# A gated cross-attention and MoE block on one core: sums of squares moved to ScalarE, unread products at the start, front work reordered

## The reference

```
x = x + tanh(g_xattn) * xattn(layernorm(x), ctx_2048, desc_router, W_q, b_q, itok)
x = x + tanh(g_ffn)   * moe(layernorm(x), gate_w, gate_b, fc1_w, fc1_b, fc2_w, fc2_b, alpha)

xattn: q = x @ W_q.T + b_q;  scores = q @ desc_router.T / 16, only the 4 sets listed for the token;
       the best 2 of them -> softmax weights over the 64 sets -> weights @ set_states
moe:   logits = x @ gate_w + gate_b; best 2 of 8 experts, softmax of the two, times alpha;
       for each of the 8 experts: gelu(x @ w1 + b1) @ w2 + b2, weighted and summed
layernorm(x) = (x - mean) / sqrt(var + 1e-5)
```

## Time and profile before

| | |
|---|---|
| three runs | 306.29, 307.38, 309.16 us |
| median | 307.38 us |
| profiled execution: span from the first to the last instruction | 304.3 us |
| profiled execution: time of its own beside the span | not given; the median is 3.1 us above the span |
| TensorE products busy | 251.6 us (83%) |
| VectorE busy | 213.1 us (70%) |
| ScalarE busy | 177.5 us (58%) |
| GpSimd busy | 147.2 us (48%) |
| mean granted TensorE clock | 0.907 |

### The profile page before, as it was taken

The page is one execution under the profiler, slowest core; times in us unless marked ns, Lnnn a source line. Parts: engine busy times, 40 slices in busy tenths (PEclk is TensorE's granted clock), DMA queues, the critical chain, the costliest instruction groups (busy, mean ns, idle before and its releaser), DMA issues.

```text
span 304.3 us, 9126 instructions
## 1 busy us (share of the span) xinstructions
PE 251.6 (83%) x3075; PEld 235.6 (77%) x3075; DVE 213.1 (70%) x701; ACT 177.5 (58%) x491; POOL 147.2 (48%) x122
## 2 busy tenths in 40 slices
PE   2999534241799999999999999999999999999910
PEld 2998433231689989999999999999999999989900
DVE  4899999896789778686677768677866555455500
ACT  2144878776574766856766685676666545555400
POOL 2121148994524556677545464454536355444240
PEclk9999855555599999999999999999999999999995
DMA  6999999996414444474534454455454536452320
GB/s 179 336 375 377 378 371 378 377 322 214 106 34 77 73 72 70 73 83 80 97 63 74 88 74 80 80 77 69 77 84 74 87 55 94 69 77 32 37 31 3
DMA packets 47262, 41.06 MB, mean 135 GB/s; under 512 B 23569, under 2 KB 43794, under 8 KB 47090
## 3 DMA queue, kind: packets, MB, share of 16 engines
q1 hardware_dynamic: 39088, 29.75, 33.0%
q0 software_dynamic: 7488, 10.39, 23.1%
q10 hardware_dynamic: 642, 0.33, 0.4%
HBM read 26.10 MB, written 9.37 MB: 117 GB/s over the span
## 4 chain that ended last, share of the span: by engine, by line
PE 60%; DVE 12%; DMA 6%; issue 3%; ACT 3%; POOL 1%; DVEq 0%; POOLq 0%; ACTq 0%
PE bank L615 30%; PE bank L631 29%; DMA out_dram<-xn,add_at 4%; DMA xs<-xrows,fetch_at 1%; DVE rows L1052 1%; DVE wreg L1061 1%; DMA xTp<-xs 1%; ACT wreg L806 1%; ACT rows L877 1%; DVE xs L1031 1%; DVE earlier L1105 1%; DVE wreg L1297 1%; DVE gmark L1095 1%; POOL out_dram L1529 1%; POOL xs L1521 1%
## 5 line engine op out<-in xcount | busy, mean ns | idle before, releaser
L615 PE MATMUL bank<-xTp,wreg 128*128 128x128 f16 x1872 | 155.3, 221 | 1.4 <-ACT xTp L866 0.7
L631 PE MATMUL bank<-wreg,rows 128*128 x936 | 150.5, 273 | 0.3 <-DVE rows L1434 0.3
L615 PEld LDWEIGHTS bank<-xTp,wreg 128*128 x1872 | 131.1, 99 | 9.6 <-issue 1.4
L877 ACT ACTIVATE rows<-bank,maskbias 128x128 f32<-128x128 f32 x312 | 88.9, 371 | 42.1 <-PE bank L615 21.6
L1529 POOL DMA_INDIRECT out_dram<-xn,add_at x39 | 66.7, 1711 | 88.1 <-DMA out_dram<-xn,add_at 48.8
L631 PEld LDWEIGHTS bank<-wreg,rows 128*128 128x128 f16 x936 | 79.1, 98 | 4.3 <-issue 0.4
L1432 DVE TENSOR_SCALAR rows<-rows 128x512 f16<-128x512 f32 x78 | 36.5, 468 | 41.6 <-ACT rows L877 41.5
L1521 POOL DMA_INDIRECT xs<-xrows,fetch_at x39 | 47.1, 1206 | 23.2 <-issue 11.3
L1434 DVE SCALAR_TENSOR_TENSOR rows<-rows 128x512 f16<-128x512 f32 x78 | 54.0, 693 | 2.7
L1297 DVE SCALAR_TENSOR_TENSOR wreg<-wreg (+1 forms) x16 | 36.7, 2292 | 13.9 <-ACT wreg L806 13.3
L885 ACT ACTIVATE xn<-xn,maskbias 128x256 f32<-128x256 f32 x39 | 20.0, 513 | 36.9 <-DVE xn L1423 36.8
(11 more groups left out here) (202 smaller groups left out, 208.0 us busy)
## 6 DMA issues: line engine op xcount, KB each, us to landing
wreg<-in_L_ffn_fc_w_dram SPq DMA_DIRECT2D x16, 1024.0 KB, 12.7
xrows<-rows SPq DMA_DIRECT2D x4, 528.0 KB, 6.4
xs<-in_x_dram SPq DMA_DIRECT2D x4, 512.0 KB, 9.3
out_dram<-xs SPq DMA_DIRECT2D x4, 512.0 KB, 9.1
xs<-in_L_ffn_fc_b_dram SPq DMA_DIRECT2D x1, 1024.0 KB, 5.7
xs<-xrows,fetch_at POOLq DMA_INDIRECT x39
out_dram<-xn,add_at POOLq DMA_INDIRECT x39
xTp<-xs SPq DMA_TRANSPOSE x38, 3.2
```

Source lines behind the costliest of these rows:

```text
L615: mm = pe.matmul(put, w, xT[:, i % NX, x_part, k, :], start=(k == 0 and n == 0), stop=(k == KC - 1 and n == 2))
L631: mm = pe.matmul(yb, h, w, start=(c == 0 and n == 0), stop=(c == FC - 1 and n == 2))
L877: op = act.activation(h32[i % 2][:, f * P:(f + 1) * P], bank[2 * (i % 2) + half][:, c * P:(c + 1) * P], ACT.Gelu, bias=b1cur[:, i % NX, f: ...
```

## The change

1. `norm1` is kept for group 0 alone. For groups 1 to 3 ScalarE runs a new `spread(g)`: four activations Square of the raw rows with bias minus the mean (from `xgate`) and the sum along the row into `var_sum`; VectorE's `variance1(g)` makes (sum + 256 eps)/256 of it in one operation. The power on GpSimd stays.
2. The minus mean comes from `xgate`, so `keep_gate` is moved ahead: for groups 1 to 3 it waits for the score products only, no longer for VectorE's reading of the bank. `score_pair(3, 0)` now waits for that reading instead.
3. TensorE starts with 20 products of `ones` (f16 view, 256 columns) into bank 3, which nobody reads; they wait for the memset of `ones`.
4. The context transposes go to banks 6 and 7 instead of 5 and 6, and TensorE waits for the mask only before attention(0).
5. The order of calls on TensorE, ScalarE and VectorE is another; on VectorE `norm1(0)` comes after the projection's part of `rhs_c`, and `variance1` and `weigh_sets(2)` are put between the halves of `add_attention`.

```diff
+        var_sum = sb("var_sum", [P, NT])
...
+        UNREAD = 20
...
             def score_pair(g, j):
...
-                if g >= 2 and j == 0:
-                    pe.wait_ge(xgate_ready, g - 1)
+                if g == 2 and j == 0:
+                    pe.wait_ge(xgate_ready, 2)
+                if g == 3 and j == 0:
+                    pe.wait_ge(scores_read, 2)
...
+            pe.wait_ge(ones_ready, 2)
+            for n in range(UNREAD):
+                pe.matmul(bank[3][:, 0:2 * P], ones[:, 0:P // 2].bitcast(F16), ones[:, :].bitcast(F16), start=True, stop=True)
             pe.wait_ge(pool_const, 1)
...
             pe.wait_ge(ctx_in, 16)
-            pe.wait_ge(mask_ready, 1)
             transpose_sets(0)
             score_pair(1, 0)
             transpose_sets(1)
+            score_pair(1, 1)
             transpose_pair(2, 0)
-            score_pair(1, 1)
+            transpose_pair(2, 1)
             pe.wait_ge(ctxT_sb, 2)
             set_gates((0, 1))
             score_pair(2, 0)
             set_gates((2, 3))
-            transpose_weights(0)
-            transpose_pair(2, 1)
-            attention(0)
             score_pair(2, 1)
             transpose_pair(3, 0)
             transpose_pair(3, 1)
+            transpose_weights(0)
+            pe.wait_ge(mask_ready, 1)
+            attention(0)
+            score_pair(3, 0)
+            score_pair(3, 1)
             transpose_weights(1)
-            score_pair(3, 0)
             attention(1)
-            score_pair(3, 1)
             transpose_weights(2)
...
             def keep_gate(g):
-                act.wait_ge(scores_read, g + 1)
+
+                if g == 0:
+                    act.wait_ge(scores_read, 1)
+                else:
+                    act.wait_ge(pair_used, 2 * g + 2)
...
+            def spread(g):
+
+                act.wait_ge(xgate_ready, g + 1 if g >= 2 else 1)
+                for t in range(GT):
+                    n = g * GT + t
+                    act.activation(xn[:, 1, t, :], xs[:, n, :], ACT.Square, bias=xgate[:, g, t, E:G1],
+                                   accum_out=var_sum[:, n:n + 1]).then_inc(var_ready, 1)
...
             copy_pair(0, 0)
             copy_pair(0, 1)
-            act.wait_ge(gates_in, 16 * 2)
-            act.activation(tg[:, :], gcol[:, :], ACT.Tanh).then_inc(gates_ready, 1)
             copy_pair(1, 0)
             copy_pair(1, 1)
             copy_sets(0)
+            copy_sets(1)
+            keep_gate(1)
+            spread(1)
             keep_gate(0)
-            set_exp(0)
-            copy_sets(1)
             copy_pair(2, 0)
+            copy_pair(2, 1)
             act.wait_ge(ctxgw_ps, 1)
             act.activation(ctxgw[:, :, 0:G1], bank[7][:, 2 * P:2 * P + NG * G1].rearrange("n (m e) -> n m e", e=G1),
                            ACT.Copy).then_inc(ctxgw_sb, 1)
-            copy_weights(0)
-            copy_pair(2, 1)
-            keep_gate(1)
-            set_exp(1)
+            set_exp(0)
+            act.wait_ge(gates_in, 16 * 2)
+            act.activation(tg[:, :], gcol[:, :], ACT.Tanh).then_inc(gates_ready, 1)
             copy_pair(3, 0)
             copy_pair(3, 1)
+            copy_weights(0)
+            keep_gate(2)
+            spread(2)
+            set_exp(1)
             copy_weights(1)
+            keep_gate(3)
+            spread(3)
+            squares(0)
             set_exp(2)
-            squares(0)
-            keep_gate(2)
             copy_weights(2)
...
-            norm1(0)
             v.wait_ge(proj_ps, 1)
...
+            norm1()
             v.wait_ge(itok_in, 16)
...
-            norm1(1)
...
             pick_sets(0)
-            norm1(2)
+            variance1(1)
             weigh_sets(0)
             pick_sets(1)
-            norm1(3)
+            add_attention(0, lambda: variance1(2))
             weigh_sets(1)
-            add_attention(0)
             pick_sets(2)
-            weigh_sets(2)
-            add_attention(1)
+            variance1(3)
+            add_attention(1, lambda: weigh_sets(2))
             variance2(0)
```

More of the change, by code:

```diff
@@ L133, in flamingo_block @@
         stats = sb("stats", [P, GT, 6])
-        mv1 = sb("mv1", [P, NT, 2])
+        mv1 = sb("mv1", [P, GT, 2])
         ve1 = sb("ve1", [P, NT])
@@ L278, in flamingo_block @@
         set_ones = sem("set_ones")
+        var_ready = sem("var_ready")
         ve1_ready = sem("ve1_ready")
@@ L444, in transpose_sets @@
                         c = (m % 2 * KC + k) * P
-                        mm = pe.transpose(bank[5 + h][:, c:c + P], ctx_sb[:, m, k * P:(k + 1) * P], ident[:, :])
+                        mm = pe.transpose(bank[6 + h][:, c:c + P], ctx_sb[:, m, k * P:(k + 1) * P], ident[:, :])
                 mm.then_inc(ctxT_ps, 1)
@@ L716, in copy_sets @@
                 act.wait_ge(ctxT_ps, h + 1)
-                act.activation(ctxT[:, 2 * h:2 * h + 2, :, :].rearrange("p m k n -> p (m k n)"), bank[5 + h][:, :],
+                act.activation(ctxT[:, 2 * h:2 * h + 2, :, :].rearrange("p m k n -> p (m k n)"), bank[6 + h][:, :],
                                ACT.Copy).then_inc(ctxT_sb, 1)
             def keep_gate(g):
-                act.wait_ge(scores_read, g + 1)
+                if g == 0:
+                    act.wait_ge(scores_read, 1)
+                else:
+                    act.wait_ge(pair_used, 2 * g + 2)
                 act.activation(xgate[:, g, :, :], bank[2 + g % 2][:, 0:GT * NR].rearrange("p (t n) -> p t n", t=GT)[:, :, NS:NR],
                                ACT.Copy).then_inc(xgate_ready, 1)
+            def spread(g):
[4 more added lines that the diff above has]
+                                   accum_out=var_sum[:, n:n + 1]).then_inc(var_ready, 1)
             def set_exp(g):
@@ L840, in _ @@
             normalise(0)
-            keep_gate(3)
             copy_weights(3)
@@ L902, in _, with norm1, variance1 @@
             done = Count()
-            def norm1(g):
-                v.wait_ge(x_in[g], 16)
+            def norm1():
+                v.wait_ge(x_in[0], 16)
                 for t in range(GT):
-                    v.bn_stats(stats[:, t, :], xs[:, g * GT + t, :]).then_inc(vec_step, 1)
+                    v.bn_stats(stats[:, t, :], xs[:, t, :]).then_inc(vec_step, 1)
                 v.wait_ge(vec_step, done.up(GT))
                 for t in range(GT):
-                    v.bn_aggr(mv1[:, g * GT + t, :], stats[:, t, :]).then_inc(vec_step, 1)
+                    v.bn_aggr(mv1[:, t, :], stats[:, t, :]).then_inc(vec_step, 1)
                 v.wait_ge(vec_step, done.up(GT))
+                v.tensor_scalar(ve1[:, 0:GT], mv1[:, :, 1], EPS, None, ALU.add).then_inc(ve1_ready, 1)
+            def variance1(g):
                 r = slice(g * GT, (g + 1) * GT)
-                v.tensor_scalar(ve1[:, r], mv1[:, r, 1], EPS, None, ALU.add).then_inc(ve1_ready, 1)
+                v.wait_ge(var_ready, g * GT)
+                v.tensor_scalar(ve1[:, r], var_sum[:, r], D * EPS, 1.0 / D, ALU.add, ALU.mult).then_inc(ve1_ready, 1)
             v.memset(ones_d[:, :], 1.0 / D).then_inc(ones_ready, 1)
-            v.memset(ones[:, :], 1.0).then_inc(vec_step, 1)
+            v.memset(ones[:, :], 1.0).then_inc(ones_ready, 1)
             v.memset(ctxgw[:, :, G1:G2], 1.0).then_inc(set_ones, 1)
@@ L929, in _ @@
             v.tensor_copy(ident_h[:, :], ident[:, :]).then_inc(ident_ready, 1)
-            v.wait_ge(vec_step, done.up(10))
+            v.wait_ge(vec_step, done.up(9))
             v.tensor_scalar(region[:, :], iota64[:, 0:E], float(CAP), None, ALU.mult).then_inc(vec_step, 1)
@@ L1013, in weigh_sets, with add_attention @@
                                        op0=ALU.is_equal, op1=ALU.mult).then_inc(wset_ready, 1)
-            def add_attention(g):
+            def add_attention(g, between=None):
                 gates = bank[4][:, 2 * P:2 * P + GT * G2].rearrange("p (t e) -> p t e", t=GT)
@@ L1026, in add_attention @@
                 for j in range(2):
+                    if j == 1 and between:
+                        between()
                     v.wait_ge(attn_ps, 2 * g + j + 1)
@@ L1035, in add_attention @@
                         v.wait_ge(gate_read, g + 1)
-                        v.wait_ge(xgate_ready, g + 1)
+                        v.wait_ge(xgate_ready, max(g + 1, 2))
                         v.tensor_tensor(ugate[:, g, :, :], ugate[:, g, :, :], xgate[:, g, :, :], ALU.add).then_inc(ugate_ready, 1)
```

## The result

The changed kernel took 312.25 us (median of 20 runs, 307.99 to 314.63), the kernel before in the same series 306.54 us (20 runs, 305.35 to 309.16). The two medians lie 5.7 us apart, 1.9%. So part of what is left out belongs to the change, and 1.2% is the smaller reading.

The account below looks back on a forecast made before the run. The front, up to the list of rows to gather, was taken as the bound: VectorE gains 6.6 us but waits 7.7 instead of 0.6, shift +0.5. Span 304.3 + 0.5 = 304.8, median 3.1 above: 307.9 us, range 304.2 to 311.3.

Parts of the forecast that it names:

- Unread products: TensorE's start: 20 products take 4.3 us, end as the first rows land, lose nothing and lift the clock.
- rival D: TensorE's front: the unread products don't lift the clock, half speed until 18.8 us; +5.7, 313.1 us; chance 0.08.
- pick_sets(0): VectorE's front: this call starts at 13.1 us instead of 16.00, 2.9 us won.
- The squares and their queue: ScalarE's squares, 1.96 us a group, delay set_exp; VectorE waits 1.9, 3.6 and 1.3 us, though rid of 5.5 us.
- From 5.5 us on I take the full clock.: TensorE in the front: every step from 5.5 us on is laid out at 2.4 GHz, transposes 1.0 instead of 1.9 us.
- Rival B: TensorE's front: clock falls again in thin stretches (9 to 11 or 16 to 18 us); +2.1 to +3.8 us; chance 0.22.
- whatever the change gives or takes before that moves the end of the kernel by as much.: List of rows to gather, 73.05 us: any shift of the front ahead of it reaches the kernel's end in full.
- Size of the order's own cost: End of VectorE's front: variance2(0) at 34.55 us instead of 34.07, 0.5 us later than in the kernel before.
- Rival C: VectorE's list bounds the front, ScalarE is in time; saving capped at 3.4 us by the DMA; 304.0 us; chance 0.18.

Follow-up runs that it names:

- e6: Changed kernel with unread products in every gap of TensorE's front (4, 6, 12, 6, 10, 5, 30) to hold the clock; 307.62 us, ratio 1.0061 to the kernel before.
- e10: e6 with set_exp(2) moved ahead of squares(0) on ScalarE; 306.68 us, ratio 0.9998 to the kernel before.
- e11: e6 with the three spread calls gone and norm1(1) to norm1(3) on VectorE where variance1 stood; 308.85 us, ratio 1.0070 to the kernel before.
- e4: Changed kernel plus 12 unread products ahead of score_pair(2, 0) and 8 ahead of transpose_weights(1); 309.04 us, ratio 1.0068 to the kernel before.
- e5: Kernel before plus 20 unread products at the start and more in every gap of the front; 306.41 us, ratio 1.0011 to the kernel before.
- e9: e6 plus 16 unread products ahead of the first gathered rows and 16 between the first two expert tiles; 308.75 us, ratio 1.0071 to the kernel before.
- e8: e5 plus 16 unread products ahead of the first gathered rows and 16 between the first two expert tiles; 304.94 us, ratio 0.9982 to the kernel before.
- e12: e8 with 30 unread products instead of 16 ahead of the gathered rows and 8 behind their transposes; 306.04 us, ratio 0.9962 to the kernel before.
- e1: Kernel before plus only the change's 20 unread products at the start; 307.88 us, ratio 0.9969 to the kernel before.
- e3: Changed kernel with set_exp(2) moved ahead of squares(0) on ScalarE; 314.81 us, ratio 1.0217 to the kernel before.
- e7: Changed kernel with only group 3's squares on ScalarE, a third order of calls and unread products in the gaps; 310.49 us, ratio 1.0101 to the kernel before.
- e2: Changed kernel without the 20 unread products; 315.65 us, ratio 1.0279 to the kernel before.

## Why the prediction was wrong in its likeliest case, and how near its rival came

The forecast was 307.9 us, 0.5 over the kernel before, and a change within 1% had 0.73. It came out 1.2% slower. The range, up to 311.3, just held the ratio (1.0119 times 307.38 is 311.0) and did not hold the raw median.

- *Unread products.* 4.3 us forecast, 4.45 measured, done at 5.70 before the rows at 5.95. Right, with some luck: in the kernel before the rows were there at 5.49. That they lift the clock: right (rival D falls), but at 7.0 us, not 5.5; the rows' eight transposes took 1.55, not 1.0.
- *pick_sets(0)* at 13.92 for 13.1: 0.8 late by that clock and by rows and gate weights that landed 0.4 to 0.5 later.
- *The squares and their queue.* The times are right: four squares in 1.96 us; score (2, 0) at 18.36 for 18.2, the set gates done at 20.3 for 20.1, weigh_sets(0) at 21.57 for 21.3, VectorE's wait 3.72 for 3.6; the wait before weigh_sets(2) 1.22 for 1.3. Only the wait for the squares of group 1 was 1.07 for 1.9, as pick_sets(0) came late. That VectorE's savings turn into waits on ScalarE is what e6 (3.72 and 1.36 with the clock held) and e10 show. But that the first of them is the squares' doing is not shown: without them e11 waits 3.40 at the same place, and what holds set_exp(0) there is its place behind the copy of the set gates.
- *The step that failed*: "From 5.5 us on I take the full clock." Between weigh_sets(0) and add_attention(0) the changed kernel took 4.64 us where I had 3.3, because scores and transposes ran at 1.2 GHz from 20.6 to 24.1; with the clock up there it is 3.43 (e4 and e6). From there to variance2(0) it is 10.0 us, as laid out (9.95). So variance2(0) came at 36.24 for 34.55, and 1.2 of the 1.7 us are this fall. Rival B named it, with the place (a thin stretch at 16 to 18 us), the reason (a fall behind a stretch that isn't full) and a price of 2.1 to 3.8. I gave it 0.22. The fall came at 20.6 us, later than B had it (18 us, and in any case before 20). B's price is that of the front, where 2.2 us over before are measured at variance2(0) and 2.7 at the list of rows. That the time is 3.65 over before, inside its 2.1 to 3.8, is in part luck: the rest was lost behind the front, at a place it doesn't name. The row that spoke for it, TensorE 3.93 us busy of 5 ahead of the fall at 36, should have weighed more: the forecast itself has TensorE waiting for its input until 18.2.
- *"whatever the change gives or takes before that moves the end of the kernel by as much."* Only over many runs, and not at one to one. This step failed too. The change's list of rows came 2.7 us late and the span grew by 5.1, since the second tile's rows arrived late and the clock fell again at 88.9 us; whether that is the change's doing or this execution's alone stays open. e5's list came 2.2 early and nothing was won, since the rows' stores weren't in. Of e9's 3.4 over e8, at least 2.1 reached the end by the medians, 1.0 by the ratios. One execution gives the end of the front; it doesn't give the end of the kernel to better than 2 us.
- *Size of the order's own cost.* I had +0.5 at variance2(0) against a kernel before that has the late clock. That comparison is right in kind, but hides how bad the order is: against an old order that has the early clock too (e5) it is 3.4 at variance2(0). The products are the part that pays for it.
- *Rival C* falls: VectorE did wait on ScalarE. Its cap, the landing of the rows, is real (e5).

The Trainium skill ("TensorE: Matmul & The Clock Gate", Part 1) says that idling brings the throttle back. The changed kernel's fall at 20.6 us, with 1.38 us of idle TensorE ahead of it, can be read that way; e12's fall, with TensorE busy 4.99 us of 5 in the stretch ahead, doesn't.

## What to carry to other kernels

When work is moved from a full engine to one that looks idle, read the second engine's queue and not its share: what stands ahead of the work that the full engine needs next (here the exponentials) decides, and the saving turned into waits of 3.7 and 1.2 us. It need not be the moved work itself: the longer wait stayed at 3.4 us with the squares gone (in part behind 12 unread products), since a copy that waits for TensorE stood ahead of the exponentials too. Change who does a piece of work and the order of the calls one at a time. A clock lifted early by unread products has to be held through the thin places that the faster TensorE opens, or it is lost where it counts and the times scatter. Judge such a change with the clock held on both sides, old order and new, and keep in mind that the products that hold it stand in the queue as well.

## What the runs showed of the hardware that I had not expected

- The fall of the clock in the front is not tied to one schedule. e5, e8 and e12 have the same products up to 70 us; in two of the three profiled executions the clock held to 36 us, in the third it fell at 21.5. In e1, e3, e7 and the changed kernel it fell at 19.0 to 20.6, each time within about 3 us of the gate products of only 9 columns. These products can't be the whole cause: the kernel before and e5, e6, e8, e9, e10 and e11 ran the same ones with the clock up, and it didn't fall behind them.
- In e1 the time goes with the mean granted clock: its executions run from 303.24 us at 0.899 to 312.67 at 0.866; e4's lie, all but one, at 0.894 to 0.901, and their range is 5.8 us where e1's is 9.4.
- With twenty f16 products of 256 columns from 1.25 us on the clock was up by 7.0 us (4.5 to 7.3 in the traces of the eleven kernels that have them besides); before, TensorE had worked from 5.5 us on and the clock rose at 18.8, and in e2 at 16.1.
